# Neighbourhood attention block: loop written out, operations moved between the slots of a band, two PSUM bank lists exchanged

## The reference, cut to what matters

```python
def _arsinh_norm(x, w, b):
    return w * jnp.arcsinh(x) + b
...
h1 = _arsinh_norm(h, n1_w, n1_b)
h = h + _na2d(h1, qkv_w, qkv_b, proj_w, proj_b)     # q k v, scores with 9 neighbours, softmax, proj
h2 = _arsinh_norm(h, n2_w, n2_b)
ff = jax.nn.gelu(h2 @ mlp_w1 + mlp_b1, approximate=False) @ mlp_w2 + mlp_b2
return h + ff
```

## Time and profile before

| what | value |
|---|---|
| median of 3 runs | 4895.31 us |
| profiled execution, its own time | 4905.26 us |
| its span on the engines | 4903.5 us |
| PE, DVE, ACT, POOL busy, share of the span | 89%, 76%, 68%, 82% |
| granted TensorE clock, mean | 0.975 |
| DMA moved | 600.50 MB, 122 GB/s |

### The profile page before, as it was taken

How to read it: one execution, slowest core, us unless ns; L and a number is a source line. 1 busy time by engine, 2 the same in 40 slices (tenths; PEclk the granted TensorE clock), 3 DMA queues, 4 the chain that set the end, 5 groups by cost and what they waited for, 6 DMA issues and landing times.

```text
span 4903.5 us, 149526 instructions
## 1 busy us (share of the span) xinstructions
PE 4361.5 (89%) x53320; PEld 3118.8 (64%) x53320; DVE 3743.8 (76%) x7717; ACT 3345.0 (68%) x4865; POOL 4044.6 (82%) x5498
## 2 busy tenths in 40 slices
PE   3899899999999989999999989989999998999997
PEld 2666666666666666666666666666666666666665
DVE  4777777877777777778777778777777777787784
ACT  2676677777677666767767667676776767677674
POOL 1788888888888888888888888888888888888885
PEclk9999999999999999999999999999999999999998
DMA  3454444444444444444445444444544444454441
GB/s 79 127 130 121 124 127 127 125 127 125 123 130 126 122 125 126 126 124 130 125 122 130 121 127 126 125 124 123 131 126 122 129 123 124 122 131 125 121 124 54
DMA packets 593557, 600.50 MB, mean 122 GB/s; under 512 B 76558, under 2 KB 540560, under 8 KB 590352
## 3 DMA queue, kind: packets, MB, share of 16 engines
q1 hardware_dynamic: 592912, 591.32, 46.2%
HBM read 197.69 MB, written 135.40 MB: 68 GB/s over the span
## 4 chain that ended last, share of the span: by engine, by line
POOL 47%; issue 32%; PE 15%; ACT 3%; POOLq 1%; DVE 1%; SPq 1%; DMA 0%; ACTq 0%; DVEq 0%
PE ps L384 15%; POOL p_lo L1055 9%; POOL b_lo L1074 8%; POOL g_lo L1084 7%; POOL g_hi L1082 6%; POOL k_win L1102 5%; POOL gate L1049 5%; POOL b_hi L1072 3%; POOL k_win L1112 2%; ACT p_hi L991 2%; POOL k_win L1121 1%; ACT L1000 1%; POOLq L1052 0%; ACT prob L990 0%; POOL a_lo L1064 0%
## 5 line engine op out<-in xcount | busy, mean ns | idle before, releaser
L1055 POOL TENSOR_TENSOR p_lo<-prob,p_hi 100x512 f16<-100x512 f32 x1024 | 1347.4, 1330 | 272.7 <-ACT p_hi L991 272.7
L990 ACT ACTIVATE prob<-ps 100x512 f32<-100x512 f32 x1024 | 615.7, 601 | 960.8 <-PE ps L384 959.7
L818 DVE TENSOR_REDUCE ps<-ps 128x8 f32<-128x800 f32 x512 | 510.5, 997 | 280.4 <-PE ps L384 280.4
L1049 POOL TENSOR_TENSOR gate<-gate_in 1x1 f32<-1x1 f32 x894 | 285.9, 320 | 492.2 <-DVE ln_u L744 434.3
L849 DVE TENSOR_TENSOR o_norm<-ps,recip 64x128 f32<-64x128 f32 x2048 | 591.4, 289 | 52.1
L1084 POOL TENSOR_TENSOR g_lo<-g,g_hi 128x512 f16<-128x512 f32 x512 | 591.9, 1156 | 41.0
L991 ACT ACTIVATE p_hi<-ps 100x512 f16<-100x512 f32 x1024 | 617.7, 603 | 0.0
L384 PEld LDWEIGHTS ps<-v_win,p_hi 100*128 100x128 f16 x8192 | 483.8, 98 | 181.5 <-issue 16.0
L384 PE MATMUL ps<-w_hi,g_hi 128*128 128x256 f16 x2048 | 560.8, 274 | 0.0
L384 PE MATMUL ps<-w_lo,g_hi 128*128 128x256 f16 x2048 | 560.7, 274 | 0.0
L384 PE MATMUL ps<-w_hi,g_lo 128*128 128x256 f16 x2048 | 560.6, 274 | 0.0
(11 more groups left out here) (105 smaller groups left out, 12397.6 us busy)
## 6 DMA issues: line engine op xcount, KB each, us to landing
keys<-k_win SPq DMA_DIRECT2D x1536, 100.0 KB, 2.2
v_win<-v_rows SPq DMA_DIRECT2D x1024, 101.6 KB
queries<-q_nat SPq DMA_DIRECT2D x1536, 64.0 KB
v_rows<-v_nat SPq DMA_DIRECT2D x256, 260.0 KB, 4.5
xin<-in_x_dram SPq DMA_DIRECT2D x128, 512.0 KB, 4.0
out_dram<-y SPq DMA_DIRECT2D x256, 256.0 KB, 2.7
queries<-in_query_mask_dram SPq DMA_DIRECT2D x128, 160.0 KB
keys<-in_mlp_w_dram SPq DMA_DIRECT2D x2, 512.0 KB, 6.2
```

Of the source, the lines that this page charges most:

```text
L818: v.tensor_reduce(maxima_of_pair(), ps[:, B_S:B_S + 2, 0:PAIRS * NK].rearrange("p n (a k) -> p n a k", k=NK), AX.X, ALU.max).then_inc(max3 ...
L990: act.activation(prob[b][0:NK], ps[0:NK, B_ST + b, :], ACT.Exp, scale=INV * INV).then_inc(prob_ready, 1)
L1049: pool.tensor_tensor(gate[:, n:n + 1], gate_in[:], gate_in[:], ALU.add)
L1055: pool.tensor_tensor(p_lo[b][0:NK], prob[b][0:NK], p_hi[b][0:NK], ALU.subtract).then_inc(p_lo_ready, 1)
```

## The change

- `run` has one loop over all steps in the program text: -3 to 129, written out; no hardware loop, and every semaphore count is a constant.
- `pass_waits` and its tiles are gone; the waits stand directly ahead of the first real operation. One fewer tile is zeroed at the start.
- X_BANK goes from [1, 2] to [1, 0], V_BANK from [0, 1] to [2, 1]. On PE, `v_product(t + 2, 0)` goes between the two halves of `x_transposes`. The waits for a bank's last reader follow: the second transposes wait for the second q_low instead of the first, v_product's first half for the first instead of the second, the first half of mlp_out for v_low, its second half for the second xT.
- DVE: the magnitude of norm 2 goes from k = 1 to the end of k = 0; the sign of norm 2 ahead of the magnitude of norm 1 in k = 2; the sum of norm 1 ahead of the first half of y, and the second half of y behind the normalisation of tile 5; the sign of norm 1 in k = 3 from behind `maxima_to_rows` to behind `o_low`, ahead of the reciprocal of tile 6.
- ACT: `o_high(t - 1, 1)` goes between the probabilities of tiles 0 and 1; the last logarithm of norm 1 from k = 3 to the end of k = 2.
- POOL: the second `windows_main` goes from between the p_low of tiles 4 and 5 to behind `b_parts`.

```diff
-X_BANK = [1, 2]
-V_BANK = [0, 1]
+X_BANK = [1, 0]
+V_BANK = [2, 1]
...
-            for t in range(-3, XT):
-                step(t, t % XT)
-            with eng.Fori(0, BANDS // XT - 2) as i:
-                for n in range(XT):
-                    step(i * XT + (XT + n), n)
-            for t in range(BANDS - XT, BANDS + 2):
+            for t in range(-3, BANDS + 2):
                 step(t, t % XT)
...
-                    pe.wait_ge(q_lo_ready, signals(t - 1, G, 1))
+                    pe.wait_ge(q_lo_ready, signals(t - 1, G, 2))
                 for k in range(BLOCKS):
                     s = pe.transpose(ps[:, X_BANK[g], k * P:(k + 1) * P], xin[:, k, g * P:(g + 1) * P], ident[:])
...
             def v_product(t, n):
 
                 if n == 0:
-                    pe.wait_ge(q_lo_ready, signals(t, G, 2))
+                    pe.wait_ge(q_lo_ready, signals(t, G, 1))
...
             def mlp_out(t, par, n):
...
-                    if has(t + 5):
-                        pe.wait_ge(xT_ready, signals(t + 5, G, 2))
-                    elif has(t + 4):
-                        pe.wait_ge(q_lo_ready, signals(t + 4, G, 1))
+                    if has(t + 4):
+                        pe.wait_ge(v_lo_ready, signals(t + 4, 2, 1))
...
                         x_transposes(t + 3, 0)
+                    if k == 1 and pre:
+                        v_product(t + 2, 0)
+                    if k == 1 and fill:
                         x_transposes(t + 3, 1)
                     if k == 1 and pre:
-                        v_product(t + 2, 0)
                         v_product(t + 2, 1)
...
@@ DVE
-                    if k == 1 and post:
-                        magnitude2(t - 1, old)
                     if k == 1 and pre:
                         q_low(t + 2, par, 0)
+                    if k == 2 and post:
+                        sign2(t - 1, old)
                     if k == 2 and fill:
                         magnitude1(t + 3, (u + 3) % XT)
-                    if k == 2 and post:
-                        sign2(t - 1, old)
                     if k == 3 and att:
                         o_low(t, par, 0)
+                    if k == 3 and fill:
+                        sign1(t + 3, (u + 3) % XT)
...
-                    if k == 2 and fin:
-                        result(t - 2, 0)
                     if k == 2 and fill:
                         sum1_(t + 3)
                     if k == 2 and fin:
-                        result(t - 2, 1)
-                    if k == 3 and fill:
-                        sign1(t + 3, (u + 3) % XT)
+                        result(t - 2, 0)
 
                     if att:
                         sum_reciprocal(t, 2 * k + 1)
                         normalise(t, 2 * k + 1)
+                    if k == 0 and post:
+                        magnitude2(t - 1, old)
                     if k == 1 and pre:
                         v_low(t + 2, 1)
+                    if k == 2 and fin:
+                        result(t - 2, 1)
@@ ACT
                         probabilities(t, 2 * k)
+                    if k == 0 and post:
+                        o_high(t - 1, old, 1)
...
                         probabilities(t, 2 * k + 1)
-                    if k == 0 and post:
-                        o_high(t - 1, old, 1)
...
                         root(ln1_s[:], ln1a, root1, t + 3)
-                    if k == 3 and fill:
                         log1_(t + 3)
@@ POOL
                 pool.wait_ge(pe_v, signals(t - 1, 2, 2))
-                pass_waits(0)
...
                         p_low(t, 2 * k)
-                    if k == 2 and pre:
-                        windows_main(t + 2, par, 1)
-                    if att:
                         p_low(t, 2 * k + 1)
...
                         b_parts(t - 1)
+                    if k == 2 and pre:
+                        windows_main(t + 2, par, 1)
```

More of the change, by code:

```diff
@@ L51 @@
 N_LOADS = 14 + 2 * PAIRS
-N_ZERO = 12
+N_ZERO = 11
 V_BV, V_ALL = 1, 23
@@ L140, in build @@
         b2 = sb("b2", [P, C], F32)
-        gate_in, gate = sb("gate_in", [1, 1], F32), sb("gate", [1, 7], F32)
         xin = sb("xin", [P, BLOCKS, C], F32)
@@ L440, in k_product @@
                 elif g == 0:
+                    pe.wait_ge(xT_ready, signals(t, G, 1))
                     pe.wait_ge(v_lo_ready, signals(t - 1, 2, 2))
                     pe.wait_ge(o_lo_ready, signals(t - 3, 2, 1))
-                else:
-                    pe.wait_ge(xT_ready, signals(t, G, 2))
                 for kg in range(G):
@@ L456, in q_product @@
                 else:
-                    pe.wait_ge(v_lo_ready, signals(t - 1, 2, 1))
+                    pe.wait_ge(xT_ready, signals(t, G, 2))
                 for kg in range(G):
@@ L490, in turn @@
                 else:
-                    pe.wait_ge(v_lo_ready, signals(t + 2, 2, 1))
+                    pe.wait_ge(xT_ready, signals(t + 3, G, 2))
                 for n in range(TILES // 2):
@@ L516, in mlp_in @@
                 elif m == 0:
-                    pe.wait_ge(xT_ready, signals(t + 4, G, 2))
+                    pe.wait_ge(v_lo_ready, signals(t + 3, 2, 1))
                 elif m == 1 and has(t - 1):
@@ L520, in mlp_in @@
                 elif m == 1:
-                    pe.wait_ge(v_lo_ready, signals(t + 3, 2, 1))
+                    pe.wait_ge(xT_ready, signals(t + 4, G, 2))
                 elif m == 2 and has(t + 1):
@@ L538, in mlp_out @@
                     pe.wait_ge(g_lo_ready, signals(t, MT, MT))
-                    if has(t + 5):
-                        pe.wait_ge(xT_ready, signals(t + 5, G, 2))
-                    elif has(t + 4):
-                        pe.wait_ge(q_lo_ready, signals(t + 4, G, 1))
+                    if has(t + 4):
+                        pe.wait_ge(v_lo_ready, signals(t + 4, 2, 1))
                     else:
                         pe.wait_ge(gelu_ready, signals(t, MT, 4))
+                elif has(t + 5):
+                    pe.wait_ge(xT_ready, signals(t + 5, G, 2))
                 elif has(t + 4):
-                    pe.wait_ge(v_lo_ready, signals(t + 4, 2, 1))
+                    pe.wait_ge(q_lo_ready, signals(t + 4, G, 2))
                 elif has(t + 1):
@@ L679, in _ @@
             zero(k_nat[:].rearrange("p l g r j -> p (l g r j)"))
-            zero(gate_in[:])
             zero(v_nat[:, 1].rearrange("p a w -> p (a w)"))
@@ L1045, in _ @@
             pool.wait_ge(zeroed, N_ZERO)
-            def pass_waits(n):
-                pool.tensor_tensor(gate[:, n:n + 1], gate_in[:], gate_in[:], ALU.add)
             def p_low(t, c):
@@ L1069, in b_parts @@
                 pool.wait_ge(pe_m1, signals(t - 1, MT, MT))
-                pass_waits(1)
                 for g in range(G):
@@ L1079, in g_parts @@
                 pool.wait_ge(pe_m2, signals(t - 1, 2, 2))
-                pass_waits(2 + ms[0] // 2)
                 for m in ms:
@@ L1097, in windows_main @@
                     pool.wait_ge(k_in[par], landed(t - 2, K_DMAS))
-                    pass_waits(4)
                 for g in range(G):
@@ L1108, in windows_bottom @@
                 pool.wait_ge(k_lo_ready, signals(t + 1, G, G))
-                pass_waits(5)
                 for lo in range(2):
@@ L1117, in windows_top @@
                 pool.wait_ge(k_in[par], landed(t - 2, K_DMAS))
-                pass_waits(6)
                 for lo in range(2):
```

## The result

The changed kernel takes 4491.05 us (4486.94 to 4494.16), against 4895.11 before (median of 4 runs here, 4895.31 of 3 in the table above): a ratio of 0.917 (95% interval 0.915 to 0.919), 404 us less. These are the median and the range of three runs; a fourth, which took 12871.03 us at a granted clock of 0.33, is left out (with it the median would be 4492.6). The forecast was 4545, with 4405 to 4740 around it. The profiled execution is the one of 4491.05 us.

What follows compares the result with a forecast made beforehand. A ring of waits, no single engine, was taken to set the 36.03 us band. 1.73 a band over about 124 bands (215) plus the loop's 135 make 350 off 4905.26: 4555, less 10 for the median, 4545; range 4405 to 4740.

Steps and rivals of the forecast that it cites:

- The loop's 135: Loop written out: 29 surcharges where the loop closes go, 135 us over the run, bounds 105 and 145.
- The ring: Waits from a_parts over PE, p_low, b_parts, mlp_in, weighted(6), DVE and sign1 to a_parts set the 36.03 us band.
- The walk's first leg: After k_product's start K: p_hi(5) at K+18.7, then p_low(5) 1.16 plus 1.45 for sign2 and magnitude1, ending K+21.3.
- the banks' exchange: V and x banks exchanged: 0.75 of PE's 1.00 gap before v_product goes; p_hi(5) at K+18.7 instead of 19.4.
- the gates: Seven one-element POOL additions a band, 0.13 each, removed: gain 0 to 0.9; those ahead of a_parts and b_parts count.
- near ties: POOL's chain (34.15) and PE's own time (34.05) end within 0.1 of each other, so the band was taken as 34.3.
- What is late next: With the a_lo and b_lo stalls gone, p_lo(6) delays weighted(6) by about 0.6, and again a_lo by a hair.
- Key copies: Second key-window copies, 1.37 us on POOL, moved behind b_parts: saves nothing of POOL's sum, makes no DMA later.
- A: Rival: PE becomes the bound, sign1 fitting beside POOL; band 33.4, time 4435; chance 0.20.
- the prediction's own sign: Forecast is wrong if the band stays over 35.5 (B) or PE has no gap over 0.3 anywhere (A).
- B: Rival: only the loop is gained, POOL and DVE blocking each other; band 35.5 to 36.0, 4700 to 4760; chance 0.20.
- C: Rival: slower, straight code stalls on its own instruction fetch, 3.6 us in every band; 5005; chance 0.06.

Runs made afterwards that it cites:

- the new order: The changed kernel with the hardware loop and the seven gates (`pass_waits`) put back, new order and banks kept: 4661.45 us, steady band 34.27.

## Why the prediction was right, step by step

*The kinds of time.* Right: one steady band and a surcharge at 29 places. The loop's 135 was measured at 132 (interval 124 to 140). Its lower bound, 105, counted PE's stops alone; the rest is above all the longer work at the lower granted clock behind them, which the prediction didn't name (PE busy 34.78 at 0.96 against 33.23 at 1.00).

*The ring.* Its mechanism was right: the sign of x behind PE closed it, and moving it is the largest part (0.97 of 2.19; 1.26 alone). What the blocking of POOL by a two-input operation costs was right too (0.97 forecast, 0.98 measured), and it cut the right way against the idle 2.74. The rule of the Trainium skill quoted there ("SBUF — State Buffer", section "Who interferes with whom"), that the loser fully blocks, was priced at the whole length of each operation and put at 35.1; the terms listed add up to 35.3. The band of 33.84 agrees with the smaller price of the rows. The blocking itself is full, as the rule has it: in the kernel before, the changed one and every run here, p_low(5) ends 1.02 behind the end of the sign of h (1.01 to 1.03 over the bands between 1900 and 2900 us), though it takes anything from 1.35 to 2.14. The price is less than the operation's length because the loser has to sit out only what is left of it, and about 0.14 of its own 1.16 runs beside it. An added operation of two inputs cost 1.12 a band and one of one input 0.14.

*The walk's first leg* named the wrong releaser. It ran from p_hi(5), K+18.7, over p_low(5) with 1.16 + 1.45. In the trace p_low(5) is timed by the sign of h on the DVE, which lies behind sum, v_low and maximum and ends at K+19.6. It had p_low(5) end at K+21.3, which measured K+20.6; the 0.48 for the magnitude of x fell on b_hi behind it (1.07 instead of 0.60), and the sum of x took 0.99 for 0.90. The number was near by luck, 25.8 for the end of b_parts against 25.7: in this order the sign of h starts only 0.4 ahead of p_low(5), so that nearly all of it stands in p_low(5)'s way. Therefore the banks' exchange, credited with 0.7 through p_hi(5), measured 0.25, and the gates, 0.26 in the walk, measured 0.53. Two wrong terms of opposite sign.

*Later legs* were forecast at 27.2 (copies), 30.5 (p_low(7)) and 34.1 (a_lo); they are 27.0, 30.2 and 33.8. The 0.15 added for near ties was not needed. So the mis-sized term of the sum is the band, 34.3 for 33.84: 0.46 x 124 = 57 us, 0.31 of it the walk's, 0.15 the allowance. With the loop's 132 for 135 it explains the 54 us between 4545 and 4491.

*What is late next.* Right in place, p_lo before weighted(6), half in size (0.29 for 0.6). a_lo by a hair is right too: k_product starts 0.06 behind its end, with 0.07 of idle time on PE.

*Key copies.* Priced at nothing, measured 0.05. The gather of V was read wrong and without effect: it starts at K+24.1 before, not 23.5, and at K+25.2 after; PE waited for it once in the run, 2.3 us. *magnitude of h, order of sign and magnitude, y, the o eviction:* each priced 0 to 0.3; not tried singly, and they stay open. The four groups taken back singly sum to 0.53 + 0.97 + 0.25 + 0.05 = 1.80 of 2.19; what is left, 0.39, is theirs or comes from the groups acting together.

*The rivals.* A, PE's bound, was nearer than its 0.20 said: 33.84 lies between the forecast's 34.3 and A's 33.4, and one more move reaches it (33.38). By the prediction's own sign the steady band even counts as A: no gap of PE is over 0.3 in it, the largest is 0.29. The sign doesn't tell the two apart. The time lies in the forecast's range of 4475 to 4650, but the band of 33.84 is a little under its 33.9 to 34.9. B and C are refuted, B by the steady band, C by the run with the loop alone.

## What to carry to other kernels

A ring that several engines close is found by asking of each operation on it what times its end, not what it waits for at its start: p_low(5) was released by ACT and finished by the DVE, and only the second mattered. An engine that is 93% busy need not be the bound by its sum, even where part of its work is on the ring: taking 2 us a band off POOL's first half gave 0.08, moving a 0.7 us operation of the DVE, which was 85% busy, gave 0.46. Take one part back at a time before believing a sum, since the terms of this one were off by 0.45 and 0.27 in opposite directions and the total hid it.

## What the runs showed of the hardware

- Where the loop closes, a closing cost 4.5 us (132/29; by the bands' mean 4.6, in the new order 4.1), of which PE's idle time without a releaser is 3.6 (3.3). Behind the stop the granted clock fell to 0.50 (1.2 GHz) for some microseconds in all 28 closings looked at before, and in 18 of 28 in the new order; without the fall a closing cost 2.8 us there, with it 4.4 or 5.7. Waits against a register instead of a constant cost nothing measurable: 36.03 and 36.01.
- A DVE operation with two SBUF inputs and a POOL operation run one behind the other, and either can be the one that waits: p_lo 2.13 instead of 1.16 where the DVE came first, the sign 2.17 instead of 1.24 where POOL did. In all fourteen traces p_lo ended 1.02 behind the sign's end however long it had waited; where the sign is the one that waits, it ended 1.08 behind p_lo's end. Each is its own length alone (1.16 and 1.22) less 0.14. A reduction with a single SBUF input that writes one column (1.21 us) disturbed nothing; the magnitude, with a single SBUF input too but writing a whole tile, did (b_hi 1.07 instead of 0.60).
- POOL's addition of one element is held up in the same way: 0.64 us with the gates put back, 1.17 before, instead of 0.18.
